# Reordering the work inside one pipelined step of a cross-attention and FFN layer: mix first, a W1 tile ahead of the query products, statistics ahead of the inversion, exponentials split up

## The reference, cut to what matters

```python
n   = layernorm(x)
q   = n @ Wq + bq                       # 16 heads of 16
s   = einsum(q, k) / 4; s = where(mask == 0, -1e9, s)
a   = softmax(s) @ v                    # 64 keys, k and v shared by the heads
x   = x + a.reshape(...) @ Wo + bo
n   = layernorm(x)
m   = k0*n[t-1] + k1*n[t] + k2*n[t+1]   # "mix"
h_p = m @ W1[p] + b1[p]                 # 9 paths of 64
g   = argmax(tanh(m @ Wo1 + bo1) @ Wo2 + bo2)
out = x + layernorm(n + (h_g @ W2[g] + b2[g])) * gamma + beta
```

## Time and profile before

| | us |
|---|---|
| median of 3 runs | 399.33 (394.64 to 399.48) |
| profiled execution, its time | 401.61 |
| profiled execution, its span | 399.8 |
| PE busy in the span | 342.2 (86%) |
| DVE / ACT / POOL busy | 276.9 / 166.2 / 186.4 |
| start of ST0 in steps (1,0), (1,1), (2,0) | 97.73, 140.47, 185.17 |
| start of ST0 in steps (2,1), (3,0), (3,1) | 228.32, 271.18, 311.88 |
| mean granted clock of PE | 0.948 |

### The profile page before, as it was taken

How to read it: one execution, slowest core, us unless ns; L and a number is a source line. 1 busy time by engine, 2 the same in 40 slices (tenths; PEclk the granted TensorE clock), 3 DMA queues, 4 the chain that set the end, 5 groups by cost and what they waited for, 6 DMA issues and landing times.

```text
span 399.8 us, 7445 instructions
## 1 busy us (share of the span) xinstructions
PE 342.2 (86%) x2764; PEld 249.4 (62%) x2764; DVE 276.9 (69%) x622; ACT 166.2 (42%) x253; POOL 186.4 (47%) x217
## 2 busy tenths in 40 slices
PE   1587894896999999898999989898999899989990
PEld 0564472373567956686566857694678477866890
DVE  3346288488387849877489838985777854787866
ACT  1432543524545355434545364434651445137500
POOL 0240103201809169542939187735963397249124
PEclk9995997997899999899999999999999899989996
DMA  7308102000020002100120002000100010001003
GB/s 218 126 0 194 27 2 65 3 0 2 0 68 2 0 2 67 56 0 0 52 66 0 0 32 86 0 0 2 54 2 0 1 54 2 0 2 52 2 2 105
DMA packets 20420, 13.45 MB, mean 34 GB/s; under 512 B 10081, under 2 KB 20138, under 8 KB 20394
## 3 DMA queue, kind: packets, MB, share of 16 engines
q1 hardware_dynamic: 18754, 12.53, 10.6%
q10 hardware_dynamic: 1640, 0.57, 0.6%
HBM read 8.90 MB, written 4.19 MB: 33 GB/s over the span
## 4 chain that ended last, share of the span: by engine, by line
PE 44%; DVE 21%; issue 14%; POOL 11%; DMA 5%; ACT 4%; ACTq 1%; DVEq 0%; POOLq 0%; SPq 0%
PE ps L419 8%; PE ps L572 4%; DVE mx L1077 4%; DVE st L1024 4%; PE ps L424 3%; DMA xin<-in_x 3%; PE ps L637 3%; PE ps L527 3%; POOL x1b L1390 3%; PE ps L655 3%; POOL x L1384 2%; PE ps L660 2%; PE ps L656 2%; DMA bqs<-in_L_xattn_bq 2%; DVE osb L1095 2%
## 5 line engine op out<-in xcount | busy, mean ns | idle before, releaser
L1370 POOL TENSOR_TENSOR rs<-ve,halfneg 128x4 f32<-128x4 f32 x24 | 25.2, 1050 | 157.0 <-DVE ve L1040 157.0
L823 ACT ACTIVATE e<-ps 128x1024 f32<-128x1024 f32 x32 | 31.1, 1022 | 37.8 <-PE ps L534 37.8
L1071 DVE CAST qr<-q 128x512 fp32r<-128x512 f32 x16 | 9.4, 598 | 45.7 <-ACT q L811 45.6
L1077 DVE TENSOR_REDUCE mx<-ps 128x16 f32<-128x1024 f32 x32 | 37.8, 1210 | 0.7 <-PE ps L502 0.7
L655 PE MATMUL ps<-w2h,hmh 128*128 128x256 f32 (+1 forms) x140 | 35.8, 291 | 0.0
L656 PE MATMUL ps<-w2l,hmh 128*128 128x256 f32 (+1 forms) x140 | 34.6, 282 | 0.0
L572 PE MATMUL ps<-wo,osb 128*128 128x256 f32 x128 | 32.9, 404 | 1.6 <-DVE osb L1095 1.6
L419 PE MATMUL ps<-xmh,w1h 128*128 128x512 f32 x80 | 28.8, 443 | 6.2 <-ACT hs L867 3.9
L1421 POOL TENSOR_TENSOR hml<-hs,hmh 128x512 fp32r<-128x512 f32 x24 | 30.0, 1274 | 1.8 <-ACT hmh L877 1.7
L867 ACT ACTIVATE hs<-ps,b1s 128x512 f32<-128x512 f32 x28 | 19.4, 692 | 27.2 <-PE ps L424 27.1
L1384 POOL TENSOR_TENSOR x<-xin,bos 128x256 f32<-128x256 f32 x32 | 28.3, 914 | 0.7 <-POOL x1b L1390 0.3
(11 more groups left out here) (154 smaller groups left out, 822.1 us busy)
## 6 DMA issues: line engine op xcount, KB each, us to landing
xin<-in_x SPq DMA_DIRECT2D x8, 512.0 KB, 3.7
out<-y SPq DMA_DIRECT2D x7, 512.0 KB, 2.9
min_<-in_mask_Bx1xSxS_ik SPq DMA_DIRECT2D x8, 128.0 KB, 3.6
cst<-in_constants SPq DMA_DIRECT2D x1, 660.5 KB, 10.8
hs<-in_L_ffn_W SPq DMA_DIRECT2D x2, 288.0 KB
hs<-in_L_ffn_W SPq DMA_DIRECT2D x1, 512.0 KB
out<-xin SPq DMA_DIRECT2D x2, 256.0 KB, 2.2
cst<-in_constants SPq DMA_DIRECT2D x1, 384.0 KB, 5.7
```

What stands on the lines that cost most here:

```text
L823: nc.scalar.activation(e[:, 2 * i:2 * i + 2, :], ps[:, bank:bank + 2, :], ACT.Exp).then_inc(s_e, 1)
L1077: v.tensor_reduce(mx[:, k, :].rearrange("p (a h) -> p a h", a=2), ps[:, bank:bank + 2, :].rearrange("p a (h s) -> p a h s", s=SK), AX.X, A ...
L1370: g.tensor_tensor(ln[7][:, :], ln[6][:, :], halfneg[:, :], ALU.pow).then_inc(s_r, 1)
```

## The change

Five things are written in another order, in the steps with a feed-forward part:

1. PE: the W1 product of tile 0 stands between ST0 and `wq` and no longer behind ST1.
2. ACT: the four exponentials are no longer in one piece. After two of them come `hidden` of tile 0 and the copies of q, after the third `hidden` of tile 4, after the fourth `hidden` of tile 1. The high halves of the mixed input come ahead of `pv_copy` and no longer behind all `hidden`.
3. DVE: the mix is the first work of a step, ahead of the rounding of q.
4. DVE: `layernorm1_stats(after)` stands ahead of `invert`.
5. DVE: in `last_column` the wait for POOL's low halves (s_earlyl) stands ahead of the rounding to xmh, one instruction earlier.

```diff
@@ PE step
                 if n:
                     scores_transposed(*n, 0, front)
+                if f:
+                    w1(*f, 0)
                 if front:
                     wq(*front, fb)
                 if n:
                     scores_transposed(*n, 1, front)
                 if f:
-                    w1(*f, 0)
                     w1(*f, 4)
@@ ACT softmax_exp
-            def softmax_exp(b, j):
-                act.wait_ge(s_dn, at(b, NJ, j))
-                for i in range(4):
+            def softmax_exp(b, j, quarters):
+                if quarters[0] == 0:
+                    act.wait_ge(s_dn, at(b, NJ, j))
+                for i in quarters:
@@ ACT step
                 if n:
-                    softmax_exp(*n)
+                    softmax_exp(*n, (0, 1))
+                if f:
+                    hidden(*f, 0)
                 if front:
                     q_copy(*front, 0 if f else 6)
-                if f:
-                    hidden(*f, 0)
+                if n:
+                    softmax_exp(*n, (2,))
+                if f:
                     hidden(*f, 4)
+                if n:
+                    softmax_exp(*n, (3,))
                 if f:
                     hidden(*f, 1)
-                if n:
-                    pv_copy(*n)
-                if f:
-                    hidden(*f, 2)
-                    hidden(*f, 3)
                 if f and f[1] == 0:
                     mixed_hi(f[0], 1)
                 if f and n[1] == NJ - 1:
                     early_mixed_hi(n[0])
+                if n:
+                    pv_copy(*n)
+                if f:
+                    hidden(*f, 2)
+                    hidden(*f, 3)
@@ DVE last_column
+                dve.wait_ge(s_earlyl, at(b, KD, KD))
                 v.tensor_copy(xmh[:, :, col], xm[:, :, col]).then_inc(s_xmh, KD)
                 dve.wait_ge(s_xmh, at(b, NJ * KD, KD))
-                dve.wait_ge(s_earlyl, at(b, KD, KD))
@@ DVE step
-                if front:
-                    q_round(*front)
                 if f and f[1] == 0:
                     second_mix(f[0])
                 if f and n[1] == NJ - 1:
                     early_mix(n[0])
+                if front:
+                    q_round(*front)
                 if f:
                     argmax(*f)
-                if n:
-                    invert(*n)
                 if after and f:
                     layernorm1_stats(*after)
+                if n:
+                    invert(*n)
```

More of the change, by code:

```diff
@@ L880, in step @@
                 if n:
-                    softmax_exp(*n)
+                    softmax_exp(*n, (0, 1))
+                if f:
+                    hidden(*f, 0)
                 if front:
                     q_copy(*front, 0 if f else 6)
+                if n:
+                    softmax_exp(*n, (2,))
                 if f:
-                    hidden(*f, 0)
                     hidden(*f, 4)
+                if n:
+                    softmax_exp(*n, (3,))
                 if f:
                     hidden(*f, 1)
+                if f and f[1] == 0:
+                    mixed_hi(f[0], 1)
+                if f and n[1] == NJ - 1:
+                    early_mixed_hi(n[0])
                 if n:
@@ L893, in step @@
                     hidden(*f, 3)
[L894 to L897, removed]
                 if f:
@@ L1231, in step @@
                     early_mix(n[0])
+                if front:
+                    q_round(*front)
                 if f:
                     argmax(*f)
+                if after and f:
+                    layernorm1_stats(*after)
                 if n:
                     invert(*n)
-                if after and f:
-                    layernorm1_stats(*after)
                 if f:
```

## The result

| | before | after |
|---|---|---|
| median of the runs, us | 399.4 (394.6 to 400.5) | 414.1 (413.3 to 415.5) |
| profiled execution, us | 401.6 | 414.1 |
| its span, us | 399.8 | 412.3 |

The changed kernel is slower by a ratio of 1.0396, 95% interval 1.0331 to 1.0461. The forecast was 410.6 us, in a range of 401 to 416, with a chance of 0.70 for slower. Between the profiled executions the spans differ by 12.5 us, where the sum of the prediction said 11.3. The medians differ by 14.7, since the profiled execution of before lay above its median.

A forecast was written before the change was run, and what follows sets the result against it. The prediction took a loop from layernorm3_apply through POOL, the load of xin, statistics and PE's projection as the bound. Terms of +3.7, +3.1, +9.4, −1.9 and −3.0 summed to +11.3 us: 412.9 profiled, 410.6 as median, range 401 to 416.

The forecast's parts named there:

- The loop: Steps (1,1), (2,0), (2,1): layernorm3_apply, POOL, load, statistics, normalisation, projection and PE's rest set their length.
- the term that decides: Statistics ahead of the inversion on DVE: reciprocal behind the load wait, 2.5 us more in each of (1,1), (2,0), (2,1).
- the 4.7 to 7 given: Sign in the trace after: some 4.7 to 7 us from mb's end to the projection in place of 2.34.
- The four pieces on the path: From mb's end: reciprocal 0.95, spread 2.05, normalisation 1.21, second maximum product 0.55, about 0.1 for hand-overs: 4.86 us.
- The low clock: PE at 1.2 GHz behind each of three new waits ahead of spread: 2.2 us per step, bounds 1.6 and 3.0.
- a term taken as zero: Shift of the load by DVE's mix first: zero, bounds a tenth of a microsecond later and 2 us earlier.
- the 1.6 of the projection: Step (1,1): the projection was already slow before, 3.57 us against 1.99, so 1.6 us come off.
- Worth nothing in the middle steps: W1 tile ahead and split exponentials in (1,1), (2,0), (2,1): no gain, since PE waits ahead of spread anyway.
- (1,0): PE's W1 tile 0 waits for the last column of the mixed input: +3.7 us, bounds 1.7 and 4.0.
- (3,0): W1 tile and split exponentials remove PE's waits of 1.15 and 0.79 us: minus 1.9 us.
- (3,1) with the tail: Step (3,1): W1 tile 0 fills PE's 1.20 us wait and keeps the clock up: minus 3.0 us, bounds 1.2 and 3.9.
- no wait: Sign in the trace after: no wait at the third W1 tile, where 0.79 us had been spent waiting for ACT.

The follow-up runs named there:

- the order alone: The kernel before with only the statistics put ahead of the inversion on DVE: 409.5 us, ratio 1.0303.
- the run with PE's and ACT's part alone: The kernel before with the change's order on PE, of ACT's exponentials and in the last column; DVE's mix and inversion stay: 410.4 us, ratio 1.0304.
- the same move: The kernel before with POOL's finish put behind the two sums that free xin, nothing of the change: 396.5 us, ratio 0.9966.
- the run with the early load: The changed kernel with POOL's finish put behind the two sums that free xin: 400.0 us, ratio 1.0100.
- the last run: Changed kernel, finish behind xin's sums, old PE/ACT order without feed-forward and in (1,0), query rounding ahead of mix: 391.3 us, ratio 0.9836.

## Why the prediction was right

**The loop and the term that decides** were right. The reciprocal starts behind mb in all three middle steps, PE waits 4.9 to 5.4 us for it, the low clock follows, and from mb's end (171.40) to the projection (177.66) pass 6.26 us in place of 2.34, inside the 4.7 to 7 given (6.30 and 6.57 us in (2,0) and (2,1)). The experiments show it from both sides: the order alone makes these steps as long as the whole change does, and with an early load it costs nothing.

**Sizes in the middle steps.** The steps gave 2.6, 4.3 and 4.4 us for a predicted 3.1, 4.7 and 4.7. The four pieces on the path, put at 4.86 us, took 4.84 where the clock stayed up. The low clock was taken at 2.2 us and was worth 6.26 less 4.84, 1.4 us, in (1,1), and 1.5 and 1.7 in the next two. The load came 0.3 to 0.5 us later, a term taken as zero with 0.1 as its bound: the prediction had add_bo right, but `finish` slowed by as much as the other two sums gained, and a little more. In (1,1) 2.5 + 1.4 + 0.3 less the 1.6 of the projection makes 2.6; in (2,1) 2.5 + 1.7 + 0.3 makes 4.5, less 0.2 for a shorter transfer.

**Worth nothing in the middle steps** (the W1 tile ahead, the exponentials apart): true beside the statistics first, but without them these parts lose 1.5 to 2.0 us a step, as the run with PE's and ACT's part alone shows. The prediction's reason, that PE would wait there anyway, was right; it did not ask what one longer wait does to the clock when the reciprocal is in time.

**(1,0)**: +4.2 for +3.7, with the 3.28 us wait for the last column and the slow stretch behind it. **(3,0)**: −1.5 for −1.9; the removed waits are gone, and a new one of 0.71 us has come, as ACT's tile 4 with its tanh now stands behind the third exponential and the gate waits for it. The prediction said "no wait" there and did not follow ACT's queue. **(3,1) with the tail**: −4.1 for −3.0, but this stretch scatters: the four kernels with before's order on PE and ACT gave 85.3 to 87.9 us and the ten with the new one 83.8 to 85.2. Their means differ by 2.2 us, less than the 3.0 predicted.

**What it missed**: +3.7 us in (0,0) and (0,1). The text ahead of the prediction says that the orders change in the steps with a feed-forward part; on ACT that is wrong, since `softmax_exp(*n, (2,))` stands behind `q_copy` whether there is an f or not. Against the predicted 11.3 us the sizes take off 1.5 (+0.5 in (1,0), −0.5, −0.4 and −0.3 in the middle steps, +0.4 in (3,0), −1.1 at the end, and rounding), the missed steps add 3.7, and the head takes off 1.0: 12.5, as measured. That the total came out within 1.2 us of the sum is in part luck: 3.7 us that nobody had foreseen stand against 1.0 of the head, which the change does not touch and which scatters between 35.3 and 37.8 us in all these runs, and against a tail 1.1 better than predicted, which is scatter too by the means above. The ratio, 1.040, lies above the 1.028 that the forecast of 410.6 stands for.

## What to carry to other kernels

A wait is worth what stands behind it: before an instruction is put ahead of another on an in-order engine, ask when its input lands, not how long it takes. Here 2.5 us of statistics cost about 4.3 us a step behind a late load and nothing behind an early one, as long as the reciprocal behind them was done when PE came to `spread`; and the gains ahead of that load were waited off again. In the changed kernel the thing to move was the load's own chain, on an engine that was busy for 46% of the span; in the kernel before the same move gave 0.3%, within noise. And read a diff of a shared step function once for each kind of step that calls it.

## What the runs showed of the hardware

The waits of 3.28, 5.02, 5.38 and 4.87 us in the changed kernel were all followed by a granted clock of 0.50, 1.2 GHz. Behind short waits the clock sometimes fell and sometimes did not, with the same waits and the same work. In the run with the early load PE has the same two gaps in (1,1) (first two rows) and in (2,1) (the last two):

```profile
158.68 1.03 PE L629 MATMUL ps<-wo,thT 64*128 64x9 f32 x8 [0.71 <-ACT thT L874]
160.12 2.87 PE L554 MATMUL ps<-e,vd 128*32 128x512 f32 x16 [0.41 <-issue]
...
243.01 1.03 PE L629 MATMUL ps<-wo,thT 64*128 64x9 f32 x8 [0.71 <-ACT thT L874]
244.45 1.92 PE L554 MATMUL ps<-e,vd 128*32 128x512 f32 x16 [0.41 <-issue]
```

In (1,1) the granted clock was 0.64 on average over 160.0 to 163.4 and the value product took 2.87 us; in (2,1) it took 1.92. In the kernel before the projection took 3.57 us behind waits of 0.81 and 0.72 us in (1,1) and 1.99 behind the same waits in (2,1). One wait of 1.42 us in the last run was followed by a clock of 1.00 from 158 to 172. So a short wait's cost to the clock could not be foretold from its length here, and part of the scatter between steps and runs may lie in this; that is not shown.

VectorE's mix and GpSimd's sums slow each other, but neither stops: four sums took 3.98 us beside the mix and 2.79 to 2.81 without it, and of DVE's two instructions of L1135 the one that ran beside POOL took 0.95 us, the one that had begun before POOL's first sum 0.48.
